# Kept weights in planes of 512 numbers per partition: transfers of 2 KB pieces in place of 8 and 4 KB

## The chip, the cores and the metric

The kernel runs on one core of a Trainium2 chip. The metric is the device time of one execution in microseconds, and the median of several runs is compared.

## The reference

A transformer block in float32 on x of 2 batches x 1024 tokens x 512. Only what matters here is shown:

```python
q = (x @ Wq.T)   # 32 heads of 128; x is layer-normed
k = (x @ Wk.T)   # 8 heads
v = (x @ Wv.T)
q = _rmsnorm(q, q_norm_w); k = _rmsnorm(k, k_norm_w)
scores = jnp.einsum('bkgqd,bksd->bkgqs', qg, k) / math.sqrt(HD)
attn = jax.nn.softmax(scores + bias[None], axis=-1)   # causal, ALiBi
out = jnp.einsum('bkgqs,bksd->bkgqd', attn, v)
x = x + out @ Wo.T
x = x + SCALING * einsum('bshr,hor,bsh->bso', low, B, scores)   # LoRA mixture of 8 experts on layernorm(x)
```

## The kernel before

**Work.** A group is one key/value head with its four query heads, in one batch: 8 groups for batch 0, 8 for batch 1, 16 in all (w = 0 to 15), each over eight tiles of 128 tokens (s = 0 to 7). A group projects k and v (256 columns) and q (512 columns), forms the scores against all keys so far, takes the softmax, multiplies with the values and adds its part of the output projection to `y` in SBUF. Every product is made three times, from operands split into an upper and a lower part (`_hi`, `_lo`; `split_product`, line 1026), so weights exist in two parts as well.

**Weights.** In the first eight groups the raw weights are loaded (2 KB per row), turned by TensorE (line 1113) and split by ScalarE (`high`, line 706) and VectorE (`low`, line 898). The turned parts are `wkvT` (4 chunks x 256 numbers per partition), `wqT` and `woT` (4 x 512). Since the second batch needs them again, `keep_wkv`, `keep_wq` and `keep_wo` write each group's two parts to DRAM (`wkv_kept`, `wq_kept`, `wo_kept`), and `back_wkv`, `back_wq` and `back_wo` read them back in groups 8 to 15 in place of loading and turning. All of them are issued from ScalarE's queue, hi and then lo. In SBUF a partition's part is contiguous, 8 KB (wkv: 4 KB), and so it is in DRAM. TensorE waits for a read-back by the semaphores `wkv_back`, `wq_back` and `wo_back`; `high` waits for a write-back (`wkv_spilled` and so on) before the buffer is written over in the next group.

**Probabilities through memory.** The products with the values need the probabilities turned. Most 128 x 128 tiles are turned by TensorE. The tiles of `MEMORY_TILES` (for s = 7 these are j = 4 to 7) go another way: `send_p` (line 557) writes them to `p_bounce` in DRAM, `fetch_p` (line 568) reads one (s, j) back as four DMAs of 64 KB, one per 32 partitions, in pieces of 32 numbers (128 B), into one of three buffers `p_raw`; VectorE finishes the turn (`flip_p`, line 907), ScalarE copies the upper part (line 714) and GpSimd makes the lower (line 805). `send_p` and `fetch_p` are issued from SyncE's queue.

**Order.** Every engine follows one written list per kind of group (`PROLOGUE`, `GROUP_A` for groups 0 to 6, `BOUNDARY`, `FIRST_B`, `GROUP_B`, `LAST`), each taking from it what is its own, in order; a wait holds up all that stands behind it on that engine. The part of `GROUP_A` around the change reads:

```python
"... values.7.0 high.kv.2 "
"values.7.1 keep_wq low.kv.2 turn.p.7.2 flip_p.7.4 q.9.0 upper_p.7.4 ..."
"high.p.7.3 low.p.7.2 flip_p.7.5 fetch_p.7.7 low.p.7.3 upper_p.7.5 flip_p.7.6 lower_p.7.5 turn.q.8 high.kv.3 "
"values.7.2 high.q.8 low.kv.3 inv_k values.7.3 keep_wkv low.q.8 values.7.4 add_y.5 values.7.5 upper_p.7.6 "
"flip_p.7.7 q.9.1 lower_p.7.6 norm_k upper_p.7.7 y.6 lower_p.7.7 values.7.6 add_y.6 turn.k.0 values.7.7 ..."
```

`y.s` (line 1026 into `y_ps`, 12 products) needs `add_y` of the tile before (line 955), since `y_ps` is one buffer; `add_y.5` stands behind `flip_p.7.6` on VectorE. `load_wo`, on ScalarE's queue, stands shortly before `keep_wq` and reads 1 MB in pieces of 2 KB. The load of Wq (`wq_v`) reads for a partition four pieces of 2 KB that lie 128 rows of 2 KB apart.

Of the kernel before, what the change touches and what calls it, by code (L numbers as in the profile page):

```python
# [11 lines left out]
F32 = mybir.dt.float32  # L12
# [3 lines left out]
P = 128  # L16
# [273 lines left out]
def attention_lora_block(nc, x, Wq, Wk, Wv, Wo, q_norm_w, k_norm_w, A, B, Wr, br, out):  # L290
    NB, S, DM = x.shape
    HD = q_norm_w.shape[0]
    H = Wq.shape[0] // HD
    NG = Wk.shape[0] // HD
    G = H // NG
    NE, RK, _ = A.shape
    NT = S // P
    C = DM // P
    W512 = G * HD
# [65 lines left out]
    turned, flipped, sends = [], [], [0, 0]  # L365
# [27 lines left out]
    with ExitStack() as ctx:  # L393
# [12 lines left out]
        wqT_hi = sb("wqT_hi", [P, C, W512], F32R)  # L406
        wqT_lo = sb("wqT_lo", [P, C, W512], F32R)
        wkvT_hi = sb("wkvT_hi", [P, C, 2 * HD], F32R)
        wkvT_lo = sb("wkvT_lo", [P, C, 2 * HD], F32R)
        woT_hi = sb("woT_hi", [P, G, DM], F32R)  # L410
# [68 lines left out]
                return probs[1][:, t // 2, (t % 2) * DM:(t % 2 + 1) * DM]  # L479
            return x_source(b, t)  # L480

        wkv_kept = nc.dram_tensor("wkv_kept", [NG, 2, P, C * 2 * HD], F32).ap()
        wq_kept = nc.dram_tensor("wq_kept", [NG, 2, P, C * W512], F32).ap()
        wo_kept = nc.dram_tensor("wo_kept", [NG, 2, P, G * DM], F32).ap()

        p_bounce = nc.dram_tensor("p_bounce", [2, NT, G, P, P], F32).ap()

# [119 lines left out]
        def _(act):  # L607
# [20 lines left out]

            def keep_wkv(w):
                after(act, "low", "wkv", w + 1, 1)  # L630
                act.dma_start(wkv_kept[w + 1, 0], wkvT_hi[:].rearrange("p c n -> p (c n)").bitcast(F32)).then_inc(wkv_spilled, 16)
                act.dma_start(wkv_kept[w + 1, 1], wkvT_lo[:].rearrange("p c n -> p (c n)").bitcast(F32)).then_inc(wkv_spilled, 16)

            def keep_wq(w):
                after(act, "low", "wq", w + 1, C - 1)
                act.dma_start(wq_kept[w + 1, 0], wqT_hi[:].rearrange("p c n -> p (c n)").bitcast(F32)).then_inc(wq_spilled, 16)
                act.dma_start(wq_kept[w + 1, 1], wqT_lo[:].rearrange("p c n -> p (c n)").bitcast(F32)).then_inc(wq_spilled, 16)

            def keep_wo(w):
                after(act, "low", "wo", w, G - 1)  # L640
                act.dma_start(wo_kept[w, 0], woT_hi[:].rearrange("p c n -> p (c n)").bitcast(F32)).then_inc(wo_spilled, 16)
                act.dma_start(wo_kept[w, 1], woT_lo[:].rearrange("p c n -> p (c n)").bitcast(F32)).then_inc(wo_spilled, 16)

            def back_wkv(w):
                g = w + 1 - NG
                after(act, "turn", "kv", w, C - 1)
                act.wait_ge(wkv_spilled, 32 * NG)
                act.dma_start(wkvT_hi[:].rearrange("p c n -> p (c n)").bitcast(F32), wkv_kept[g, 0]).then_inc(wkv_back, 16)
                act.dma_start(wkvT_lo[:].rearrange("p c n -> p (c n)").bitcast(F32), wkv_kept[g, 1]).then_inc(wkv_back, 16)

            def back_wq(w):
                g = w + 1 - NG
                after(act, "q", w, NT - 1, C - 1)
                act.wait_ge(wq_spilled, 32 * NG)
                act.dma_start(wqT_hi[:].rearrange("p c n -> p (c n)").bitcast(F32), wq_kept[g, 0]).then_inc(wq_back, 16)
                act.dma_start(wqT_lo[:].rearrange("p c n -> p (c n)").bitcast(F32), wq_kept[g, 1]).then_inc(wq_back, 16)

            def back_wo(w):
                g = w - NG
                after(act, "y", w - 1, NT - 1)  # L660
                act.wait_ge(wo_spilled, 32 * NG)
                act.dma_start(woT_hi[:].rearrange("p c n -> p (c n)").bitcast(F32), wo_kept[g, 0]).then_inc(wo_back, 16)
                act.dma_start(woT_lo[:].rearrange("p c n -> p (c n)").bitcast(F32), wo_kept[g, 1]).then_inc(wo_back, 16)

            def high(w, of, *which):
                name = named(w, "turn", of, *which)
# [544 lines left out]
```

## Time and profile before

| | |
|---|---|
| median of 3 runs | 2136.99 us (2133.37 to 2137.82) |
| the profiled execution's own time | 2138.16 us |
| its span in the profile | 2136.3 us, granted TensorE clock 0.993 |
| busy: TensorE, VectorE, ScalarE, GpSimd | 98%, 63%, 54%, 44% |
| chain that ended last | TensorE 83%, VectorE 4%, issue 4%, DMA 3% |
| DMA packets | 329,095, 176.81 MB |
| q1 (issued by SyncE) | 305,264 packets, 72.41 MB, 15.3% of 16 engines |
| q10 (issued by ScalarE) | 23,664 packets, 102.25 MB, 12.8% of 16 engines |

Times in the profile are microseconds from the start of the span. PE is TensorE, DVE VectorE, ACT ScalarE, POOL GpSimd, SP SyncE; a q behind an engine's name is its queue of instructions that don't occupy the engine. "A<-B" is what an instruction writes and reads. Idle time in brackets is the engine's own before that instruction, with what ended it. A DMA packet is one contiguous piece; the four bytes that raise a semaphore at the end of a DMA on each of the 16 DMA engines are counted as a packet too. "To landing" is from the issue to the semaphore's last step.

### The profile page before, as it was taken

The numbers are of one execution on the slowest core, as the hardware profiler recorded it, in microseconds if no ns is written. First come the engines' busy times: TensorE is split into PE (matmuls) and PEld (weight loads), VectorE is DVE, ScalarE is ACT, GpSimd is POOL, SyncE is SP. The second block draws the span as 40 slices with busy tenths as digits, with TensorE's granted clock in tenths as the row PEclk, the third lists the DMA queues.
The fourth block names the chain that finished last, engine by engine and source line by source line (L and its number), as shares of the span: only waits on it lengthen the run. The fifth ranks groups of instructions, "written<-read, shape, count | busy, mean of one in ns | idle before, by whom it ended". The sixth has DMA issues, their size and how long they took to land.

```text
span 2136.3 us, 33509 instructions
## 1 busy us (share of the span) xinstructions
PE 2083.0 (98%) x11772; PEld 1786.4 (84%) x11772; DVE 1355.6 (63%) x3431; ACT 1148.2 (54%) x3314; POOL 936.1 (44%) x984
## 2 busy tenths in 40 slices
PE   7999999999999999999999999999999999999997
PEld 6888888888888888888888888888888888888885
DVE  6656656566565665658876556566566656656676
ACT  4555545555454654645445555555555555555552
POOL 3443434444444443444443544435453443545443
PEclk9999999999999999999999999999999999999998
DMA  4152141511415125051350422313041231304112
GB/s 158 64 140 75 30 130 64 154 60 40 133 54 150 60 55 157 16 154 55 110 157 7 113 70 68 101 50 92 28 107 62 67 102 50 89 30 106 44 36 73
DMA packets 329095, 176.81 MB, mean 83 GB/s; under 512 B 243800, under 2 KB 301144, under 8 KB 320736
## 3 DMA queue, kind: packets, MB, share of 16 engines
q1 hardware_dynamic: 305264, 72.41, 15.3%
q10 hardware_dynamic: 23664, 102.25, 12.8%
q8 instruction: 95, 1.56, 0.3%
q14 instruction: 72, 0.59, 0.1%
HBM read 99.11 MB, written 75.50 MB: 82 GB/s over the span
## 4 chain that ended last, share of the span: by engine, by line
PE 83%; DVE 4%; issue 4%; DMA 3%; SPq 2%; POOL 2%; ACT 2%; ACTq 0%; DVEq 0%; POOLq 0%
PE s_ps L1026 17%; PE q_ps L1026 15%; PE y_ps L1026 15%; PE o_ps L1026 15%; PE turn_ps L1113 13%; PE turn_ps L1026 5%; DMA p_raw<-p_bounce 3%; SPq L568 2%; POOL probs_odd L799 1%; PE turn_ps L1107 1%; PE y_ps L1186 1%; DVE pT_lo L898 1%; DMA p_bounce<-probs_odd 1%; DVE y L955 0%; DVE oT_lo L949 0%
## 5 line engine op out<-in xcount | busy, mean ns | idle before, releaser
L799 POOL TENSOR_TENSOR probs_odd<-probs_odd,p_inv 128x256 f32<-128x256 f32 (+3 forms) x256 | 316.4, 1256 | 326.9 <-DVE p_inv L928 326.9
L706 ACT ACTIVATE pT_hi<-turn_ps 128x512 fp32r<-128x512 f32 x464 | 271.6, 597 | 316.2 <-PE turn_ps L1113 315.9
L799 POOL TENSOR_TENSOR probs_even<-probs_even,p_inv 128x128 f32<-128x128 f32 (+3 forms) x256 | 261.8, 1044 | 386.1 <-DVE p_inv L928 386.1
L898 DVE TENSOR_TENSOR pT_lo<-turn_ps,pT_hi 128x512 fp32r<-128x512 f32 x464 | 314.6, 684 | 146.2 <-ACT pT_hi L706 145.2
L921 DVE CUSTOM_DVE_ANT_0 probs_odd<-s_ps,rel 128x256 f32<-128x256 f32 (+3 forms) x256 | 209.3, 820 | 131.9 <-issue 131.4
L1026 PE MATMUL s_ps<-kT_hi,qT_hi 128*128 128x512 f32 (+3 forms) x768 | 278.7, 363 | 2.6 <-DVE kT_lo L900 1.8
L1026 PE MATMUL s_ps<-kT_hi,qT_lo 128*128 128x512 f32 (+3 forms) x768 | 262.9, 342 | 0.0
L1026 PE MATMUL s_ps<-kT_lo,qT_hi 128*128 128x512 f32 (+3 forms) x768 | 262.1, 341 | 0.0
L720 ACT ACTIVATE probs_odd<-probs_odd,neg_max 128x256 f32<-128x256 f32 (+3 forms) x256 | 211.9, 832 | 76.0 <-DVE neg_max L921 75.9
L921 DVE CUSTOM_DVE_ANT_0 probs_even<-s_ps,rel 128x128 f32<-128x128 f32 (+3 forms) x256 | 174.0, 686 | 118.0 <-issue 117.2
L1026 PE MATMUL o_ps<-pT_hi,v_hi 128*128 128x512 f32 x576 | 243.9, 423 | 1.9 <-DVE pT_lo L898 0.9
L1026 PE MATMUL q_ps<-wqT_hi,xnT_hi 128*128 128x512 f32 x512 | 220.9, 431 | 7.0 <-DVE qn L932 6.9
L1026 PE MATMUL o_ps<-pT_hi,v_lo 128*128 128x512 f32 x576 | 226.3, 393 | 0.0
L1026 PE MATMUL o_ps<-pT_lo,v_hi 128*128 128x512 f32 x576 | 226.0, 392 | 0.0
L720 ACT ACTIVATE probs_even<-probs_even,neg_max 128x128 f32<-128x128 f32 (+3 forms) x256 | 184.4, 721 | 76.6 <-DVE neg_max L921 75.7
L805 POOL TENSOR_TENSOR pT_lo<-p_raw,pT_hi 128x512 fp32r<-128x512 f32 x112 | 145.5, 1306 | 182.2 <-ACT pT_hi L714 181.5
L1026 PE MATMUL y_ps<-woT_hi,oT_hi 128*128 128x512 f32 x512 | 206.8, 404 | 18.7 <-DVE y L955 16.6
L1026 PE MATMUL y_ps<-woT_hi,oT_lo 128*128 128x512 f32 x512 | 203.2, 397 | 0.0
L1026 PE MATMUL y_ps<-woT_lo,oT_hi 128*128 128x512 f32 x512 | 202.5, 395 | 0.0
L1026 PE MATMUL q_ps<-wqT_hi,xnT_lo 128*128 128x512 f32 x512 | 201.4, 393 | 0.0
L1026 PE MATMUL q_ps<-wqT_lo,xnT_hi 128*128 128x512 f32 x512 | 200.6, 392 | 0.0
L1026 PEld LDWEIGHTS s_ps<-kT_hi,qT_hi 128*128 128x128 f32 x768 | 145.3, 189 | 22.3 <-DVE neg_max L921 2.1
(110 smaller groups left out, 4578.6 us busy)
## 6 DMA issues: line engine op xcount, KB each, us to landing
p_raw<-p_bounce SPq DMA_DIRECT2D x448, 64.0 KB, 2.3
p_bounce<-probs_odd SPq DMA_DIRECT2D x64, 256.0 KB, 2.3
wq_kept<-wqT_hi ACTq DMA_DIRECT2D x8, 1024.0 KB, 5.8
wq_kept<-wqT_lo ACTq DMA_DIRECT2D x8, 1024.0 KB, 8.4
wo_kept<-woT_hi ACTq DMA_DIRECT2D x8, 1024.0 KB, 8.1
wo_kept<-woT_lo ACTq DMA_DIRECT2D x8, 1024.0 KB, 10.2
p_bounce<-probs_even SPq DMA_DIRECT2D x64, 128.0 KB, 1.8
wqT_hi<-wq_kept ACTq DMA_DIRECT2D x8, 1024.0 KB, 4.8
```

Of the source, the lines that this page charges most:

```text
L568: sp.dma_start(p_raw[b * BLOCK:(b + 1) * BLOCK, n % RAW_TILES, :].rearrange("p (n j) -> p n j", j=BLOCK), blocks[b]).then_inc(p_fetched[n ...
L706: nc.scalar.activation(target, bank, ACT.Copy).then_inc(sems["high"], 1)
L720: nc.scalar.activation(row, row, ACT.Exp, bias=neg_max[:, s % 2, h:h + 1], scale=-1.0, accum_out=p_sum[:, s % 2, h:h + 1]).then_inc(sems[" ...
L799: nc.gpsimd.tensor_tensor(row, row, p_inv[:, s % 2, h:h + 1].to_broadcast((P, L)), ALU.mult).then_inc(sems["normalise"], 1)
L805: nc.gpsimd.tensor_tensor(pT_lo[:, r, :], p_raw[:, fetch_number[w, s, j] % RAW_TILES, :], pT_hi[:, r, :].bitcast(F32), ALU.subtract).then_ ...
L898: nc.vector.tensor_tensor(target, bank, upper.bitcast(F32), ALU.subtract).then_inc(sems["low"], 1)
L921: nc.vector.tensor_tensor_reduce(out=probs[s % 2][:, h, 0:L], in0=s_ps[:, at_col:at_col + L], in1=rel[:, S - L:S], scale=-float(slopes[w % ...
L1026: last = nc.tensor.matmul(target, a, m, start=start and i == 0 and k == 0, stop=stop and i == len(pairs) - 1 and k == 2)
L1107: last = nc.tensor.matmul(bank[:, 0:P + NE], f_x[:, t % 2, c * P:(c + 1) * P], arT[:, c, :], start=c == 0, stop=c == C - 1)
L1113: last = nc.tensor.transpose(bank[0:width, i * rows:(i + 1) * rows], source, ident[0:rows, 0:rows])
L1186: nc.tensor.matmul(y_ps[:], low_turned[:, t % 2, :], bT[:], start=True, stop=True).then_inc(sems["f_out"], 1)
```

## The change

The kept copies get another layout in DRAM: planes of 128 partitions x 512 numbers, one for each chunk of 512 numbers of a partition. A partition's part lies in four pieces of 2 KB (wkv: two pieces) that are 256 KB apart. The data in SBUF, the number of DMAs, their sizes, their places in the lists and all waits are as before.

```diff
--- before.py
+++ after.py
@@ -479,9 +479,16 @@
                 return probs[1][:, t // 2, (t % 2) * DM:(t % 2 + 1) * DM]
             return x_source(b, t)
 
-        wkv_kept = nc.dram_tensor("wkv_kept", [NG, 2, P, C * 2 * HD], F32).ap()
-        wq_kept = nc.dram_tensor("wq_kept", [NG, 2, P, C * W512], F32).ap()
-        wo_kept = nc.dram_tensor("wo_kept", [NG, 2, P, G * DM], F32).ap()
+
+        wkv_kept = nc.dram_tensor("wkv_kept", [NG, 2, C // 2, P, W512], F32).ap()
+        wq_kept = nc.dram_tensor("wq_kept", [NG, 2, C, P, W512], F32).ap()
+        wo_kept = nc.dram_tensor("wo_kept", [NG, 2, G, P, DM], F32).ap()
+
+        def pieces(kept, g, part):
+            return kept[g, part].rearrange("c p n -> p c n")
+
+        def pairs(turned):
+            return turned[:].rearrange("p (a c) n -> p a (c n)", c=2).bitcast(F32)
 
         p_bounce = nc.dram_tensor("p_bounce", [2, NT, G, P, P], F32).ap()
 
@@ -628,39 +635,39 @@
 
             def keep_wkv(w):
                 after(act, "low", "wkv", w + 1, 1)
-                act.dma_start(wkv_kept[w + 1, 0], wkvT_hi[:].rearrange("p c n -> p (c n)").bitcast(F32)).then_inc(wkv_spilled, 16)
-                act.dma_start(wkv_kept[w + 1, 1], wkvT_lo[:].rearrange("p c n -> p (c n)").bitcast(F32)).then_inc(wkv_spilled, 16)
+                act.dma_start(pieces(wkv_kept, w + 1, 0), pairs(wkvT_hi)).then_inc(wkv_spilled, 16)
+                act.dma_start(pieces(wkv_kept, w + 1, 1), pairs(wkvT_lo)).then_inc(wkv_spilled, 16)
 
             def keep_wq(w):
                 after(act, "low", "wq", w + 1, C - 1)
-                act.dma_start(wq_kept[w + 1, 0], wqT_hi[:].rearrange("p c n -> p (c n)").bitcast(F32)).then_inc(wq_spilled, 16)
-                act.dma_start(wq_kept[w + 1, 1], wqT_lo[:].rearrange("p c n -> p (c n)").bitcast(F32)).then_inc(wq_spilled, 16)
+                act.dma_start(pieces(wq_kept, w + 1, 0), wqT_hi[:].bitcast(F32)).then_inc(wq_spilled, 16)
+                act.dma_start(pieces(wq_kept, w + 1, 1), wqT_lo[:].bitcast(F32)).then_inc(wq_spilled, 16)
 
             def keep_wo(w):
                 after(act, "low", "wo", w, G - 1)
-                act.dma_start(wo_kept[w, 0], woT_hi[:].rearrange("p c n -> p (c n)").bitcast(F32)).then_inc(wo_spilled, 16)
-                act.dma_start(wo_kept[w, 1], woT_lo[:].rearrange("p c n -> p (c n)").bitcast(F32)).then_inc(wo_spilled, 16)
+                act.dma_start(pieces(wo_kept, w, 0), woT_hi[:].bitcast(F32)).then_inc(wo_spilled, 16)
+                act.dma_start(pieces(wo_kept, w, 1), woT_lo[:].bitcast(F32)).then_inc(wo_spilled, 16)
 
             def back_wkv(w):
                 g = w + 1 - NG
                 after(act, "turn", "kv", w, C - 1)
                 act.wait_ge(wkv_spilled, 32 * NG)
-                act.dma_start(wkvT_hi[:].rearrange("p c n -> p (c n)").bitcast(F32), wkv_kept[g, 0]).then_inc(wkv_back, 16)
-                act.dma_start(wkvT_lo[:].rearrange("p c n -> p (c n)").bitcast(F32), wkv_kept[g, 1]).then_inc(wkv_back, 16)
+                act.dma_start(pairs(wkvT_hi), pieces(wkv_kept, g, 0)).then_inc(wkv_back, 16)
+                act.dma_start(pairs(wkvT_lo), pieces(wkv_kept, g, 1)).then_inc(wkv_back, 16)
 
             def back_wq(w):
                 g = w + 1 - NG
                 after(act, "q", w, NT - 1, C - 1)
                 act.wait_ge(wq_spilled, 32 * NG)
-                act.dma_start(wqT_hi[:].rearrange("p c n -> p (c n)").bitcast(F32), wq_kept[g, 0]).then_inc(wq_back, 16)
-                act.dma_start(wqT_lo[:].rearrange("p c n -> p (c n)").bitcast(F32), wq_kept[g, 1]).then_inc(wq_back, 16)
+                act.dma_start(wqT_hi[:].bitcast(F32), pieces(wq_kept, g, 0)).then_inc(wq_back, 16)
+                act.dma_start(wqT_lo[:].bitcast(F32), pieces(wq_kept, g, 1)).then_inc(wq_back, 16)
 
             def back_wo(w):
                 g = w - NG
                 after(act, "y", w - 1, NT - 1)
                 act.wait_ge(wo_spilled, 32 * NG)
-                act.dma_start(woT_hi[:].rearrange("p c n -> p (c n)").bitcast(F32), wo_kept[g, 0]).then_inc(wo_back, 16)
-                act.dma_start(woT_lo[:].rearrange("p c n -> p (c n)").bitcast(F32), wo_kept[g, 1]).then_inc(wo_back, 16)
+                act.dma_start(woT_hi[:].bitcast(F32), pieces(wo_kept, g, 0)).then_inc(wo_back, 16)
+                act.dma_start(woT_lo[:].bitcast(F32), pieces(wo_kept, g, 1)).then_inc(wo_back, 16)
 
             def high(w, of, *which):
                 name = named(w, "turn", of, *which)
```

## Rows read from the trace of the kernel before

**Rows 1.** The page, part 1, whole span: busy us (share), instructions.

```profile
PE 2083.0 (98%) x11772; PEld 1786.4 (84%) x11772; DVE 1355.6 (63%) x3431; ACT 1148.2 (54%) x3314; POOL 936.1 (44%) x984
```

**Rows 2.** Who waited for whom, whole span: us, times, longest.

```profile
DVE p_raw L907 <- DMA p_raw<-p_bounce: 42.8, 18, 4.9
...
PE y_ps L1026 <- DVE y L955: 16.6, 7, 2.9
```

**Rows 3.** VectorE in time: start, us, instruction, idle before it.

```profile
160.31 0.71 DVE L907 STREAM_TRANSPOSE p_raw<-p_raw 128x512 f32<-128x512 f32 x1 [4.53 <-DMA p_raw<-p_bounce]
...
162.17 0.67 DVE L955 TENSOR_TENSOR y<-y_ps,y 128x512 f32<-128x512 f32 x1
...
949.74 0.71 DVE L907 STREAM_TRANSPOSE p_raw<-p_raw 128x512 f32<-128x512 f32 x1 [3.98 <-DMA p_raw<-p_bounce]
```

**Rows 4.** TensorE in time, the product after it.

```profile
162.99 0.47 PE L1026 MATMUL y_ps<-woT_hi,oT_hi 128*128 128x512 f32 x1 [2.58 <-DVE y L955]
```

**Rows 5.** ScalarE's queue in time, first group.

```profile
150.75 0.34 ACTq L636 DMA_DIRECT2D wq_kept<-wqT_hi  x1
...
151.12 0.45 ACTq L637 DMA_DIRECT2D wq_kept<-wqT_lo  x1
...
157.01 0.33 ACTq L631 DMA_DIRECT2D wkv_kept<-wkvT_hi  x1
```

**Rows 6.** SyncE's queue in time, same stretch.

```profile
149.69 10.57 SPq L568 DMA_DIRECT2D p_raw<-p_bounce  x6
```

**Rows 7.** DMA issues, 149.7 to 151.5, then 151.6 to 153.5: to landing.

```profile
p_raw<-p_bounce SPq DMA_DIRECT2D x1, 64.0 KB, 9.3
...
p_raw<-p_bounce SPq DMA_DIRECT2D x1, 64.0 KB, 8.7
```

**Rows 8.** DMA queues, 152.3 to 152.9: packets, MB, share of 16 engines.

```profile
q1 hardware_dynamic: 944, 0.12, 128.2%
...
q10 hardware_dynamic: 7, 0.02, 9.4%
```

**Rows 9.** DMA queues, 153.5 to 157.5.

```profile
q10 hardware_dynamic: 214, 1.62, 96.6%
q1 hardware_dynamic: 193, 0.02, 4.5%
```

**Rows 10.** DMA queues, 158.5 to 158.9.

```profile
q10 hardware_dynamic: 2, 0.01, 5.0%
```

**Rows 11.** DMA queues, 149.5 to 151.5.

```profile
q10 hardware_dynamic: 319, 0.65, 87.9%
q1 hardware_dynamic: 262, 0.03, 10.6%
```

**Rows 12.** DMA issues, whole span: count, KB each, median us to landing.

```profile
wqT_hi<-wq_kept ACTq DMA_DIRECT2D x8, 1024.0 KB, 4.8
wqT_lo<-wq_kept ACTq DMA_DIRECT2D x8, 1024.0 KB, 7.4
...
w_raw<-in_L_attn_Wq ACTq DMA_DIRECT2D x7, 1024.0 KB, 6.6
```

**Rows 13.** Read-backs and first uses in time: wkv, wq, wo.

```profile
1237.54 0.33 ACTq L648 DMA_DIRECT2D wkvT_hi<-wkv_kept  x1
...
1247.00 0.28 PE L1026 MATMUL turn_ps<-wkvT_hi,xnT_hi 128*128 128x256 f32 x1
...
1172.73 0.33 ACTq L655 DMA_DIRECT2D wqT_hi<-wq_kept  x1
...
1188.63 0.40 PE L1026 MATMUL q_ps<-wqT_hi,xnT_hi 128*128 128x512 f32 x1
...
1989.44 0.33 ACTq L662 DMA_DIRECT2D woT_hi<-wo_kept  x1
...
2003.17 0.39 PE L1026 MATMUL y_ps<-woT_hi,oT_hi 128*128 128x512 f32 x1
```

**Rows 14.** ScalarE in time, the next write to wkvT_hi.

```profile
181.93 0.60 ACT L706 ACTIVATE wkvT_hi<-turn_ps 128x512 fp32r<-128x512 f32 x1
```

## The prediction

> **What bounds the kernel now.** I read five views. First the busy times: TensorE works for 98% of the span [rows 1], so nothing that this change touches can matter unless TensorE comes to wait for it. Then who waits for whom: TensorE loses 16.6 us in seven waits at y_ps for the VectorE line that adds y_ps to y, and VectorE loses 42.8 us for the landing of p_raw [rows 2]. No wait of TensorE names a transfer of kept weights. Third, VectorE in time: in the first group it stands 4.53 us before the transpose of p_raw, and the addition to y, which is behind it in VectorE's written order, starts only at 162.17; the same stands in each of the seven groups with a write-back of wq, the last at 949.74 [rows 3]. TensorE's next y product starts at 162.99 after 2.58 us of idle time [rows 4]. So the seven stalls are 2.4 us each and have one cause, a fetch of the tile (s=7, j=6) that lands late.
>
> Fourth, the queues. ScalarE's queue issues the write-back of wq at 150.75 and 151.12 and that of wkv at 157.01 [rows 5], while SyncE's queue issues six fetches over 10.57 us [rows 6]. The two last quarters of the late tile land 9.3 and 8.7 us after their issues at 149.69 and 151.55, the last one at 160.28 [rows 7]. Fifth, the packets. Until 152.9 the ScalarE queue (q10) is all but empty, and q1 moves 944 packets in 0.6 us on 16 engines, 10 ns a packet on each [rows 8]. Then from 153.5 to 157.5 q10 starts 214 packets, 16 of which are counted by their 4 bytes in a semaphore, and q1 193: one for one [rows 9]. An 8 KB packet takes 0.966 x 64 us / 198 = 312 ns, a 128 B one 13 ns, so a fetch gets one small packet per 325 ns. From 158.5 to 158.9 q10 is empty again [rows 10], and there the fetches catch up.
>
> **The change, part by part.** It changes three transfers each way, 8 KB (wkv: 4 KB) packets into 2 KB ones. 40 MiB are written and 40 MiB read; that was 12,288 packets and becomes 40,960, 28,672 more. No wait, no engine instruction and no issue is added or moved.
>
> *Packet time.* The trace has 2 KB packets beside fetches, those of the Wo load just before: from 149.5 to 151.5, 319 of q10 at 87.9% and 262 of q1 [rows 11], that is 0.879 x 32 us / 319 = 88 ns each, against 78 ns for a quarter of an 8 KB one. A round of one and one is 101 ns, and in these two us q1 got 0.82 packets for one. Sixteen 8 KB packets per engine (2 MB of wq) take 5.0 us now; sixty-four of 2 KB take 5.6 us, 0.6 us more.
>
> *The collision.* At 152.9 two quarters of the late tile are outstanding. A quarter is 64 KB in 128 B pieces, 32 per engine and one semaphore, so 66 packets per engine. Now: 16 get through beside wq's 16 packets (16 x 325 ns, to 158.1), the other 50 run alone in the gap of rows 10 at 10 ns, to 158.6; with 0.5 us from last packet to landing, which I take as an estimate from a fetch's whole 1.9 us when nothing is beside it, that is 159.1. Measured is 160.28: the slowest of the 16 engines does not finish in the gap and is caught by wkv's packets. After: 66 rounds of 101 ns are 6.7 us, to 159.6, and no gap is left, since wq's write-back itself ends at about 159.3 and wkv's is queued behind it. Landing 160.1 on an average engine; some four packets more on the slowest give 160.5. So the small packets are served four times as often, but they need all the rounds that there are, and both queues end together. Against 160.28 this is +0.2 us a group, seven times +1.5 us. Bounds: if the slowest engine now loses its 1.2 us through 8 KB packets alone and later doesn't, 159.6, -0.7 us a group, -5 us; if q1 keeps the 0.82 of rows 11, 66 packets want 80 rounds of q10, 16 of them of wkv, 80 x 88 + 66 x 13 ns = 7.9 us, landing 161.3, +1.0 us, +7 us. I take +1.5 us, the value of one for one, because rows 9 show it over the longest stretch.
>
> *What is late next.* The following tile (s=7, j=7) is fetched behind it; it lands about 0.6 us later through the longer packets. y's product and one of o stand ahead of its use on TensorE, some 5 us. Cost nothing; without that cover at most 0.6 x 7 = 4 us.
>
> *Read-backs.* The Wq load has the very pattern that they get, 2 KB pieces 256 KB apart. It lands 6.6 us after its issue, the read-back of as much in 8 KB packets 4.8, and the second of a pair 7.4 [rows 12]. From above, two such loads one after the other are 13.6 us for a pair of wq or wo, 7.0 for wkv's pair, which has half the bytes. The slack: wkv is issued at 1237.54 and first used at 1247.00, 9.5 us; wq 1172.73 to 1188.63, 15.9; wo in the last group, where it is least, 1989.44 to 2003.17, 13.7 [rows 13]. All are covered, wo by 0.1 us at the bound and by some 4 us at the likelier 9.4 (6.6, and 32 pieces of 88 ns more); if cover failed it would be one wait per group.
>
> *Write-backs of wkv and wo.* wkv_hi is written over only at 181.93 [rows 14], 25 us after its issue; the others later still. Nothing.
>
> *Issuing.* ScalarE's queue spends 0.33 and 0.45 us on a pair. It may take longer with four times the pieces, but it stands in an engine that is busy 54% of the span [rows 1]; nothing, and the case that it blocks is a rival.
>
> Sum, against the profiled execution's 2138.16 us (span 2136.3): 2138.2 + 1.5 = 2139.7. That execution is 1.2 us above the median of the runs, 2136.99, so **2138.5 us**.
>
> The Trainium skill, DMA: Bandwidth & Descriptors, Queues, rings and completion order, says that an engine drains a whole packet of some 9 to 17 descriptors from one ring before it turns to the next. By that rule four to eight turns, not 66, would bring the fetch through, and it would land without delay before and after; rows 9 disagree with it, 193 against 198 single pieces.
>
> **Rivals.**
> *Faster: the fetch slips through beside the small packets.* For it: a small packet waits 88 ns in place of 312. If q1 gets 1.3 packets for one, 66 of them need 51 of q10, 51 x 88 + 66 x 13 = 5.3 us, landing 158.7, -1.6 us a group, 2127.5; with two for one or an engine that keeps several packets in flight the tile lands before 157.9, the stall of 2.4 us is gone whole, and -16.6 us give 2120.4. Against: in neither window does q1 get more than its one. Chance 0.22.
>
> *Slower: the pieces are dearer than 88 ns.* A partition's four pieces lie 256 KB apart, and the transfer of this kind in the trace needs 1.8 us more per MB than the 8 KB one [rows 12]. Over its 32 packets per engine these are 56 ns each. With the whole of it 66 rounds last 10.4 us, landing 163.8, +3.5 us x 7 = 2161.5; with half, 2149. Against: those are reads, whose first packets come slowly, while the packets from 149.5 on took 88 ns [rows 11]; the collision has writes. It decides from 9 ns per packet on (0.6 us a group, 4.3 us). Chance 0.15.
> The Trainium skill, DMA: Bandwidth & Descriptors, Latency and other measured facts, has copies at a row pitch of 512 KB run at 207 GB/s, about half of what the packets of rows 9 move (8 KB in 312 ns on 16 engines, 420 GB/s). No row here shows a write at such a pitch.
>
> *Slower: q1 lags as in rows 11.* 0.82 packets for one, 161.3, as above: 2144. Chance 0.10.
>
> *Slower: ScalarE's issues block as SyncE's do.* Six issues of SyncE took 10.57 us [rows 6], because four quarters hold 132 pieces per engine. ScalarE will have at most 99 outstanding (a load and two write-backs). If it blocked 1.5 us in each of 24 write-backs beside loads and a third reached TensorE, +12 us, 2150. Chance 0.03.
>
> *The change doesn't do what it says*: the pieces are joined again, and nothing moves. Chance 0.02, within no change.
>
> **The numbers.** Forecast with both its bounds 0.48. A difference under 0.2%, 4.3 us, can't be told from none. Faster: the first rival 0.22, less 0.02 that falls inside, and 0.02 of the forecast's lower bound: 0.22. Slower: 0.15 + 0.10 + 0.03, and the forecast's upper edge is mostly inside: 0.28. The rest, 0.50. The range takes in the first rival at its half (2127.5) and a little more, and the second at its half (2149): 2125 to 2150.
>
> **What would show it.** In the changed profile: 2 KB packets alone in q10, 28,672 more of them; between the starts of the wq write-back and its end q1 and q10 one for one at about 100 ns a round, some 5.5 to 6.5 us long; no empty q10 before wkv's packets; the tile's last quarter landing 8.5 to 9.5 us after its issue (now 8.7); TensorE's waits at y_ps still seven, 14 to 20 us in sum; p_raw's wait on VectorE 38 to 50 us; read-backs landing 6 to 7 and 9 to 10 us after issue with no wait on them. I am wrong if the seven stalls shrink below 10 us or grow over 25, if TensorE waits for a read-back, or if ScalarE's issues last over 1 us.

## The result and the profile after

The changed kernel takes 2141.8 us (median of 20 runs, 2137.26 to 2145.53) against 2137.96 for the kernel before (20 runs, 2133.37 to 2143.22): a ratio of 1.0018 [1.0011, 1.0026], 3.8 us more. The brackets hold the 95% interval, which leaves out 1, so the loss is small but clear of the noise. The forecast was no change that can be told, with +1.5 us as its sum. The profiled execution took 2139.75 us (span 2137.9).

Line numbers are 7 higher than before: the split product is L1033, the addition to `y` L962, `flip_p` L914, `fetch_p` L575. Four lines of the page of the changed kernel: busy times, the packets of the whole span, and the two queues:

```profile
PE 2080.4 (97%) x11772; PEld 1784.0 (83%) x11772; DVE 1356.4 (63%) x3431; ACT 1149.1 (54%) x3314; POOL 936.1 (44%) x984
...
DMA packets 357767, 176.81 MB, mean 83 GB/s; under 512 B 243800, under 2 KB 301144, under 8 KB 357600
...
q1 hardware_dynamic: 305264, 72.41, 15.4%
q10 hardware_dynamic: 52336, 102.25, 13.5%
```

q10 has 52,336 packets in place of 23,664, which is the 28,672 more that were counted, for the same bytes; its share of the 16 engines rises from 12.8% to 13.5%.

Who waited for whom, changed kernel (us in total, times, longest):

```profile
DVE p_raw L914 <- DMA p_raw<-p_bounce: 46.0, 22, 5.5
...
PE y_ps L1033 <- DVE y L962: 20.1, 7, 3.5
```

These answer to [rows 2]: the same seven stalls of TensorE, 20.1 us in place of 16.6, so +3.5 us. No line names a read-back.

VectorE and then TensorE in time, first group (start, us, instruction, idle before it), to be read against [rows 3, 4]:

```profile
159.38 0.71 DVE L914 STREAM_TRANSPOSE p_raw<-p_raw 128x512 f32<-128x512 f32 x1 [5.01 <-DMA p_raw<-p_bounce]
...
161.24 0.68 DVE L962 TENSOR_TENSOR y<-y_ps,y 128x512 f32<-128x512 f32 x1
```

```profile
162.06 0.64 PE L1033 MATMUL y_ps<-woT_hi,oT_hi 128*128 128x512 f32 x1 [3.34 <-DVE y L962]
```

The chain is the old one: VectorE stands before the transpose of the late tile, 5.01 us in place of 4.53, the addition waits behind it, and TensorE loses 3.34 us in place of 2.58. The seven stalls of after are 3.34, 3.50, 2.76, 3.28, 3.13, 2.11 and 2.03 us, those of before 2.58, 2.95, 2.46, 2.91, 1.79, 1.87 and 2.03.

The landing explains them. Measured from the issue of wq's write-back, which takes out that the groups start at other times, the late tile's last quarter lands after 10.3, 10.5, 9.7, 10.2, 10.1, 9.1 and 9.0 us (mean 9.83), before after 9.5, 9.9, 9.4, 9.9, 8.7, 8.8 and 9.0 (mean 9.32). That is 0.51 us a group, 3.6 us for seven: the 3.5 us of the wait.

The landing of the write-back itself goes with it. In every group the late quarter lands just behind wq's lower half: 0.34 to 0.51 us behind it in the kernel before, 0.15 to 0.35 us in the changed one. That half lands a mean 8.93 us after the first half's issue before and 9.64 after, 0.71 later. So in both kernels the fetch ends when the write-back does.

Two queues of the changed kernel, first group: 151.9 to 156.9, then the first and the last 2.5 us of it, and the microsecond behind (packets, MB, share of 16 engines):

```profile
q10 hardware_dynamic: 919, 1.84, 94.9%
q1 hardware_dynamic: 771, 0.10, 12.9%
...
q10 hardware_dynamic: 476, 0.95, 98.5%
q1 hardware_dynamic: 233, 0.03, 8.4%
...
q10 hardware_dynamic: 443, 0.89, 91.4%
q1 hardware_dynamic: 538, 0.07, 17.4%
...
q1 hardware_dynamic: 1092, 0.14, 87.8%
q10 hardware_dynamic: 83, 0.15, 38.9%
```

A 2 KB packet takes 0.985 x 2.5 x 16 us / 476 = 83 ns. Over the whole collision q1 gets 771 packets for 919, 0.84 for one. But the share isn't even: 0.49 in the first half, 1.2 in the second. Then there is a gap in q10 before wkv's packets, and q1 makes up for much of it there, with 1,092 packets in 1 us.

The kernel before is as uneven, which the average of [rows 9] hides. These are its queues from 153.5 to 155.0 and from 155.0 to 157.5:

```profile
q10 hardware_dynamic: 74, 0.61, 96.8%
q1 hardware_dynamic: 31, 0.00, 3.3%
...
q10 hardware_dynamic: 140, 1.02, 96.4%
q1 hardware_dynamic: 162, 0.02, 5.3%
```

Read-backs and write-backs (DMA issues, whole span: count, KB, median us to landing):

```profile
wq_kept<-wqT_hi ACTq DMA_DIRECT2D x8, 1024.0 KB, 6.0
wq_kept<-wqT_lo ACTq DMA_DIRECT2D x8, 1024.0 KB, 9.3
...
wqT_hi<-wq_kept ACTq DMA_DIRECT2D x8, 1024.0 KB, 5.8
wqT_lo<-wq_kept ACTq DMA_DIRECT2D x8, 1024.0 KB, 8.4
...
wkvT_hi<-wkv_kept ACTq DMA_DIRECT2D x8, 512.0 KB, 3.6
wkvT_lo<-wkv_kept ACTq DMA_DIRECT2D x8, 512.0 KB, 4.5
```

wq's read-back is 1.0 us later in each half than in [rows 12]. It has 15.9 us of slack [rows 13].

A second cost shows in the clock. Stretches of 4.5 us from a stalled y product on, of the kernel before (groups 1 and 3), then of the changed kernel (group 3); columns: us, busy time and instructions of PE, PEld, DVE, ACT, POOL, granted clock, DMA share, GB/s:

```profile
163.00:167.50 4.50, 4.50 (x13) 3.56 (x14) 1.82 (x2) 0.63 (x1) 1.52 (x2) 0.62 0.01 2
427.60:432.10 4.50, 4.49 (x21) 3.63 (x22) 2.51 (x3) 0.99 (x2) 1.56 (x2) 1.00 0.01 2
```

```profile
427.50:432.00 4.50, 4.48 (x13) 3.57 (x14) 1.82 (x2) 0.63 (x1) 1.56 (x2) 0.62 0.02 4
```

After some of the stalls TensorE runs about 3.4 us at its lower level, 1.2 GHz, and makes 13 products where it makes 21 at 2.4 GHz: 8 products of 0.22 us, 1.7 us lost beside the stall itself. Before, this followed four of the seven stalls (those of 2.58, 2.95, 2.91 and 1.87 us), after, five (the first five). So in the stretch of the seven stalls the change costs 3.5 us of waiting and 1.7 us of clock, 5.2 us. The issues of wq's write-back confirm it: from that of the first group to that of the seventh 789.98 us pass before and 794.97 after, 5.0 us more.

The two profiled executions still differ by only 1.6 us, because the kernel before was at the lower level for longer where the kernels don't differ in code. Once it was so in the first group; 40.5 to 43.9 us, before and then after, same columns:

```profile
40.50:43.90 3.40, 3.40 (x18) 3.40 (x18) 2.55 (x9) 1.47 (x5) 0.00 (x0) 0.50 1.01 417
```

```profile
40.50:43.90 3.40, 3.40 (x28) 3.17 (x28) 3.40 (x16) 2.13 (x8) 0.05 (x1) 1.00 1.03 384
```

The changed kernel issues its first group's write-back 1.7 us sooner (149.06 against 150.75). The other place is the end of the span; last 36.3 us of before and last 37.9 us of after:

```profile
2100.00:2136.30 36.30, 23.96 (x98) 15.89 (x97) 19.40 (x50) 5.79 (x14) 6.51 (x8) 0.81 0.19 52
```

```profile
2100.00:2137.90 37.90, 25.25 (x117) 17.09 (x115) 21.11 (x52) 6.96 (x16) 6.52 (x8) 0.92 0.25 60
```

(1 - 0.81) x 36.3 x 2 = 13.8 us at the lower level against (1 - 0.92) x 37.9 x 2 = 6.1 us, 7.7 us less, worth at most 3.9 us. From the seventh write-back to the end of the span the changed kernel takes 1193.9 us against 1195.6, 1.7 us less. The three parts give 5.0 - 1.7 - 1.7 = 1.6. So 3.4 us of the 5.0 were hidden in this pair by chance. The measured 3.8 us of the medians lie between 1.6 and 5.0.

### The profile page after: what moved, and what is told of

It reads as the page before. It is cut to its first block, busy times and chain, and to the rows that moved or that the text cites. A ratio compares the mean times of both kernels' runs of the same rounds, so it can differ in the third digit from the quotient of the medians.

```text
span 2137.9 us, 33509 instructions
## 1 busy us (share of the span) xinstructions
PE 2080.4 (97%) x11772; PEld 1784.0 (83%) x11772; DVE 1356.4 (63%) x3431; ACT 1149.1 (54%) x3314; POOL 936.1 (44%) x984
## 3 DMA queue, kind: packets, MB, share of 16 engines
q10 hardware_dynamic: 52336, 102.25, 13.5%
## 4 chain that ended last, share of the span: by engine, by line
PE 83%; DVE 4%; issue 4%; DMA 3%; SPq 2%; POOL 2%; ACT 2%; ACTq 0%; POOLq 0%; DVEq 0%
PE s_ps L1033 17%; PE q_ps L1033 15%; PE y_ps L1033 15%; PE o_ps L1033 15%; PE turn_ps L1120 13%; PE turn_ps L1033 5%; DMA p_raw<-p_bounce 3%; SPq L575 2%; POOL probs_odd L806 1%; DVE pT_lo L905 1%; PE turn_ps L1114 1%; PE y_ps L1193 1%; DMA p_bounce<-probs_odd 1%; DVE y L962 0%; DVE oT_lo L956 0%
## 5 line engine op out<-in xcount | busy, mean ns | idle before, releaser
L1033 PE MATMUL s_ps<-kT_hi,qT_hi 128*128 128x512 f32 (+3 forms) x768 | 278.1, 362 | 2.6 <-DVE kT_lo L907 1.8
L1033 PE MATMUL s_ps<-kT_hi,qT_lo 128*128 128x512 f32 (+3 forms) x768 | 262.4, 342 | 0.0
L1033 PE MATMUL s_ps<-kT_lo,qT_hi 128*128 128x512 f32 (+3 forms) x768 | 261.6, 341 | 0.0
L1033 PE MATMUL o_ps<-pT_hi,v_hi 128*128 128x512 f32 x576 | 243.9, 423 | 1.7 <-DVE pT_lo L905 0.9
L1033 PE MATMUL y_ps<-woT_hi,oT_hi 128*128 128x512 f32 x512 | 207.2, 405 | 22.3 <-DVE y L962 20.1
L1033 PE MATMUL q_ps<-wqT_hi,xnT_hi 128*128 128x512 f32 x512 | 220.8, 431 | 7.0 <-DVE qn L939 6.9
L1033 PE MATMUL o_ps<-pT_hi,v_lo 128*128 128x512 f32 x576 | 226.3, 393 | 0.0
L1033 PE MATMUL o_ps<-pT_lo,v_hi 128*128 128x512 f32 x576 | 226.0, 392 | 0.0
L1033 PE MATMUL y_ps<-woT_hi,oT_lo 128*128 128x512 f32 x512 | 203.6, 398 | 0.0
L1033 PE MATMUL y_ps<-woT_lo,oT_hi 128*128 128x512 f32 x512 | 203.1, 397 | 0.0
L1033 PE MATMUL q_ps<-wqT_hi,xnT_lo 128*128 128x512 f32 x512 | 201.3, 393 | 0.0
L1033 PE MATMUL q_ps<-wqT_lo,xnT_hi 128*128 128x512 f32 x512 | 200.5, 392 | 0.0
L1033 PEld LDWEIGHTS s_ps<-kT_hi,qT_hi 128*128 128x128 f32 x768 | 144.8, 189 | 22.3 <-DVE neg_max L928 2.2
## 6 DMA issues: line engine op xcount, KB each, us to landing
wo_kept<-woT_lo ACTq DMA_DIRECT2D x8, 1024.0 KB, 10.1
```

What stands on the lines that cost most here:

```text
L1033: last = nc.tensor.matmul(target, a, m, start=start and i == 0 and k == 0, stop=stop and i == len(pairs) - 1 and k == 2)
```

## The experiments

Every ratio is against the kernel before, run on the same chip beside it. "Waits at y_ps" are the seven of TensorE. The theory that came out of the result: the loss is the collision of wq's write-back with the late fetch, and the other transfers cost nothing.

**1. Which transfers cost: e1_wq_planes and e2_wkv_wo_planes.** The first puts only wq in planes, the second only wkv and wo.

```diff
--- after.py
+++ e1_wq_planes.py
-        wkv_kept = nc.dram_tensor("wkv_kept", [NG, 2, C // 2, P, W512], F32).ap()
-        wo_kept = nc.dram_tensor("wo_kept", [NG, 2, G, P, DM], F32).ap()
+        wkv_kept = nc.dram_tensor("wkv_kept", [NG, 2, P, C * 2 * HD], F32).ap()
+        wo_kept = nc.dram_tensor("wo_kept", [NG, 2, P, G * DM], F32).ap()
...
--- after.py
+++ e2_wkv_wo_planes.py
-        wq_kept = nc.dram_tensor("wq_kept", [NG, 2, C, P, W512], F32).ap()
+        wq_kept = nc.dram_tensor("wq_kept", [NG, 2, P, C * W512], F32).ap()
...
```

> Only wq's copies are in planes; wkv and wo stay contiguous (4 and 8 KB packets). Theory A (the loss is the wq write-back beside the late fetch): the whole of the change's loss or nearly, +2 to +4 us against before, the seven waits of TensorE at y_ps 19 to 20.5 us in sum, last quarter of the tile about 9.8 us after the write-back's issue. Theory B (the read-backs, or 28,672 packets spread over the run, cost it): about +1 us, in proportion to wq's share of the packets, and the seven waits stay at 16.6 us. Theory C (wkv's small packets behind catch the fetch): no loss, waits 16.6 us.

> wkv's and wo's copies are in planes, wq's stay contiguous in 8 KB packets. Theory A: no difference from before, the seven waits 16 to 17 us. Theory B: most of the loss, +2 us or more, elsewhere than in the seven waits. Theory C: the seven waits grow by 1 to 4 us, since the wkv packets that catch the slowest engine come in twice the number.

wq alone: 2141.89 us (11 runs) against 2138.28, ratio 1.0015 [1.0007, 1.0024], 3.6 us of the 3.8. wkv and wo alone: 2138.46, ratio 1.0002 [0.9993, 1.001]. Their waits at y_ps, in this order:

```profile
PE y_ps L1033 <- DVE y L962: 20.7, 7, 4.4
```

```profile
PE y_ps L1033 <- DVE y L962: 16.4, 7, 3.0
```

The loss is wq's, as far as it can be told; wkv and wo, write-backs and read-backs, were costed at nothing, and their interval reaches from -1.5 to +2.1 us. The first version's longest stall, 4.4 us, is in its first group. There the late quarter lands at 160.75, after q1 had next to nothing beside wkv's write-back, DMA queues from 158.5 to 160:

```profile
q10 hardware_dynamic: 173, 0.63, 102.1%
q1 hardware_dynamic: 14, 0.00, 0.8%
```

In its fourth group, where the stall is 3.11 us, the last quarter is issued at 548.57, between the two halves of wq's write-back (548.28 and 548.70). DMA queues from 551.3 to 553.8:

```profile
q10 hardware_dynamic: 511, 1.02, 104.7%
q1 hardware_dynamic: 17, 0.00, 0.5%
```

For 2.5 us q1 gets one packet for thirty. That isn't one for one; experiment 6 comes back to it.

**2. Is it the pitch: e3_padded_rows.** 2 KB pieces of a partition 2,304 B apart in place of 256 KB.

```diff
--- after.py
+++ e3_padded_rows.py
+        wq_kept = nc.dram_tensor("wq_kept", [NG, 2, P, C, W512 + 64], F32).ap()
...
-            return kept[g, part].rearrange("c p n -> p c n")
+            return kept[g, part][:, :, 0:W512]
```

> All copies in 2 KB pieces, but a partition's four pieces lie 2304 B apart in one row, not 256 KB apart in planes. Theory A, where only the packet's size matters: as the changed kernel, +3 to +5 us against before, seven waits near 20 us. Theory D (the distance of 256 KB makes pieces dear): as before, 16 to 17 us of waits.

2141.23 us (12 runs), ratio 1.0018 [1.001, 1.0027], the changed kernel's own; waits at y_ps 20.7 us. The distance between the pieces plays no part that can be told, only their size. The Trainium skill, DMA: Bandwidth & Descriptors, Latency and other measured facts, gives 207 GB/s for copies at a row pitch of 512 KB, 164 at 2 MB, and calls 214 the full rate of these copies; so by that page 512 KB costs little, and at 256 KB and for 2 KB pieces no loss shows here.

**3. How size counts: e5_4kb and e4_1kb.**

```diff
--- after.py
+++ e4_1kb.py
-        wq_kept = nc.dram_tensor("wq_kept", [NG, 2, C, P, W512], F32).ap()
+        wq_kept = nc.dram_tensor("wq_kept", [NG, 2, 8, P, 256], F32).ap()
...
--- after.py
+++ e5_4kb.py
-        wq_kept = nc.dram_tensor("wq_kept", [NG, 2, C, P, W512], F32).ap()
+        wq_kept = nc.dram_tensor("wq_kept", [NG, 2, 2, P, 1024], F32).ap()
...
```

> Planes of 256 numbers, so pieces of 1 KB. A packet should take some 48 ns (88 ns at 2 KB and 312 at 8 KB give 37 ns per KB and 10 fixed), a round with a small one 61 ns. Theory A with one packet for one: the wq write-back has 128 rounds per engine, and the 66 packets of the late fetch are through after 4.0 us, landing at 157.5 in the first group: the stalls vanish, -10 to -16 us against before. Theory E (what costs is the number of packets, every further one delays the fetch): the waits grow again, 24 us or more, +8 us. Theory F (the fetch gets no turn in the first 1 to 2 us of the write-back whatever the size, then one for one): waits 8 to 14 us, -3 to -8 us.

> Planes of 1024 numbers for wq and wo, pieces of 4 KB; wkv's stay one piece of 4 KB. A round is 160 + 13 ns, wq's write-back has 32 per engine and lasts 5.5 us; 32 of the 66 small packets go beside it and the rest in the gap behind. Theory A: the landing is that of the kernel before, waits 15.5 to 18 us, the time within 0.1% of before (2138). Theory E (loss grows with the number of packets): waits 18 us or more, +1 to +2 us.

| pieces | us | ratio | waits at y_ps | last quarter, mean |
|---|---|---|---|---|
| 8 KB (before) | 2138.0 | 1 | 16.6 | 9.3 |
| 4 KB | 2139.37 | 1.0006 [0.9996, 1.0015] | 18.6 | 9.6 |
| 2 KB (after) | 2141.8 | 1.0018 [1.0011, 1.0026] | 20.1 | 9.8 |
| 1 KB | 2140.17 | 1.0005 [0.9996, 1.0013] | 14.1 | 9.0 |

4 KB lies between, as a growing cost of the packets would have it; its waits are just above the 18 us of theory A, and its time can't be told from either neighbour's. 1 KB breaks the row: the fetch does get through sooner, 0.8 us of the 2 KB landing, and now 0.8 to 2.5 us before wq's lower half. But the stalls at y_ps shrink by 2.5 us against before and not by the 10 to 16 of turns one for one, and TensorE waits later in its list in return, where k is turned. This line has no counterpart in the kernel before:

```profile
PE turn_ps L1120 <- issue: 2.9, 3, 1.6
```

In the first group the stall is 1.6 us at y_ps and 1.6 us there. So what the fetch gains is lost again behind it. From the first write-back of wq to the seventh the kernel with 1 KB takes 790.0 us, that before 790.0, with 4 KB 792.5, with 2 KB 795.0 (one execution each).

**4. Move the write-backs out of the way: m_before_both and m_after_both.** `keep_wkv` goes behind `high.q.2` and `keep_wq` behind `high.p.5.0` in `GROUP_A`; the data are complete at both places. Once with the old layout, once with the new one.

```diff
--- before.py
+++ m_before_both.py
-    "values.0.0 exp.1.1 low.wkv.0 q.3.0 max.1.2 turn.q.2 invert.1.0 low.wkv.1 normalise.1.0 q.3.1 high.q.2 max.1.3 "
+    "values.0.0 exp.1.1 low.wkv.0 q.3.0 max.1.2 turn.q.2 invert.1.0 low.wkv.1 normalise.1.0 q.3.1 high.q.2 keep_wkv max.1.3 "
...
-    "scores.6.1 high.wq.3 low.wq.3 turn.p.5.0 max.6.1 turn.p.5.1 fetch_p.5.5 high.p.5.0 q.8.0 high.p.5.1 o_low.4 "
+    "scores.6.1 high.wq.3 low.wq.3 turn.p.5.0 max.6.1 turn.p.5.1 fetch_p.5.5 high.p.5.0 keep_wq q.8.0 high.p.5.1 o_low.4 "
...
-    "values.7.1 keep_wq low.kv.2 turn.p.7.2 flip_p.7.4 q.9.0 upper_p.7.4 turn.p.7.3 high.p.7.2 turn.kv.3 lower_p.7.4 "
+    "values.7.1 low.kv.2 turn.p.7.2 flip_p.7.4 q.9.0 upper_p.7.4 turn.p.7.3 high.p.7.2 turn.kv.3 lower_p.7.4 "
...
-    "values.7.2 high.q.8 low.kv.3 inv_k values.7.3 keep_wkv low.q.8 values.7.4 add_y.5 values.7.5 upper_p.7.6 "
+    "values.7.2 high.q.8 low.kv.3 inv_k values.7.3 low.q.8 values.7.4 add_y.5 values.7.5 upper_p.7.6 "
```

> The kernel before (8 and 4 KB packets) with both write-backs of the first-batch groups issued earlier in ScalarE's list, wkv's at about 50 us into the group and wq's at about 110 us, away from the fetches of s = 7. Theory A (the seven stalls are this collision): the seven waits at y_ps go from 16.6 us to under 2, and the time falls by 13 to 17 us, to about 2122. Rival G (the Wo load alone is enough to hold the fetch up): waits of 8 us or more stay, -8 us at most. Rival H (the wq write-back now delays the fetches of s = 5 and 6): a new wait of TensorE there, and less than half of the gain.

> The changed kernel (2 KB pieces) with the same two write-backs moved in the same way. Theory A: the change's loss is gone together with the stalls, so the time is that of m_before_both within 1.5 us. Theory B (2 KB pieces cost something by themselves): 3 to 5 us above m_before_both.

2111.36 us (4 runs) against 2137.28, ratio 0.9883 [0.9867, 0.9898]; with the new layout 2110.2, ratio 0.9879 [0.9865, 0.9892]. Busy times and VectorE's wait in the first of the two:

```profile
PE 2073.6 (98%) x11772; PEld 1781.5 (84%) x11772; DVE 1360.4 (64%) x3431; ACT 1149.8 (54%) x3314; POOL 942.1 (45%) x984
```

```profile
DVE p_raw L907 <- DMA p_raw<-p_bounce: 4.2, 11, 0.8
```

The wait at y_ps isn't among its lines any more, and p_raw's is 4.2 us in place of 42.8. The 26 us come out of the rows: 16.6 us of waits, and TensorE busy 9.4 us less (2083.0 to 2073.6) for the same products, 6.8 of it the clock after four stalls; the rest wasn't traced. With the collision gone the planes are 1.2 us faster (4 runs each), not slower, which shows that the loss was in the collision. Both versions beat both kernels by at least 1.2%, far more than the layout cost. The moved write-back still collides with fetches there: in the first group those of the tile s = 5 land up to 9.0 us after its issue, but nothing waits for them.

**5. Is it wkv's packets that catch the slowest engine: m_before_wkv and m_after_wkv.** Only `keep_wkv` is moved, to its place of experiment 4.

```diff
--- before.py
+++ m_before_wkv.py
-    "values.0.0 exp.1.1 low.wkv.0 q.3.0 max.1.2 turn.q.2 invert.1.0 low.wkv.1 normalise.1.0 q.3.1 high.q.2 max.1.3 "
+    "values.0.0 exp.1.1 low.wkv.0 q.3.0 max.1.2 turn.q.2 invert.1.0 low.wkv.1 normalise.1.0 q.3.1 high.q.2 keep_wkv max.1.3 "
...
-    "values.7.2 high.q.8 low.kv.3 inv_k values.7.3 keep_wkv low.q.8 values.7.4 add_y.5 values.7.5 upper_p.7.6 "
+    "values.7.2 high.q.8 low.kv.3 inv_k values.7.3 low.q.8 values.7.4 add_y.5 values.7.5 upper_p.7.6 "
```

> The kernel before, with only wkv's write-back moved early; wq's stays where it was. Theory C' (in the kernel before the slowest DMA engine is caught by wkv's packets, which is 1.2 us of each landing): the last quarter lands about 8.3 us after the wq write-back's issue in place of 9.3, the seven waits sum to 9 to 11 us in place of 16.6, -5 to -8 us. If wkv plays no part: waits 16 us, no difference.

> The changed kernel, with only wkv's write-back moved early. With theory C' and one packet for one: the fetch needs nearly all rounds of wq's write-back anyway, so it gains less than the kernel before, 0.3 to 0.7 us a group: waits 15 to 18 us, -2 to -5 us against the changed kernel (2141.8), so about 2138. If wkv plays no part: 2141.8.

2134.21 us against 2137.28, ratio 0.9992 [0.9984, 1.0001], waits at y_ps 17.3 us; with planes 2140.12, ratio 1.0013 [1.0004, 1.0022], waits 20.7. Without wkv's packets the last quarter lands 9.4 us after wq's issue in the old layout (9.3 with them), and 9.9 with planes (9.8). So on average they don't delay it, and the loss of the planes stays, 5.9 us between these two. A single group can still be hit, as the first one of e1_wq_planes was. What does go is part of p_raw's wait, 42.8 to 33.5 us, which is the next tile's, and TensorE doesn't wait for that one.

**6. What order of issue does: e6_lo_later, s_before_wq_later and s_after_wq_later.** The first issues the lower half of wq's write-back 2.5 us later, with planes. The others move the whole of `keep_wq` behind `high.p.7.3`, where both quarters of the late tile are issued ahead of it, with the old layout and with planes.

```diff
--- after.py
+++ e6_lo_later.py
-    "high.p.7.3 low.p.7.2 flip_p.7.5 fetch_p.7.7 low.p.7.3 upper_p.7.5 flip_p.7.6 lower_p.7.5 turn.q.8 high.kv.3 "
+    "high.p.7.3 keep_wqlo low.p.7.2 flip_p.7.5 fetch_p.7.7 low.p.7.3 upper_p.7.5 flip_p.7.6 lower_p.7.5 turn.q.8 high.kv.3 "
...
+                if w < 0:
+                    keep_wqlo(w)
+
+            def keep_wqlo(w):
...
--- before.py
+++ s_before_wq_later.py
-    "values.7.1 keep_wq low.kv.2 turn.p.7.2 flip_p.7.4 q.9.0 upper_p.7.4 turn.p.7.3 high.p.7.2 turn.kv.3 lower_p.7.4 "
-    "high.p.7.3 low.p.7.2 flip_p.7.5 fetch_p.7.7 low.p.7.3 upper_p.7.5 flip_p.7.6 lower_p.7.5 turn.q.8 high.kv.3 "
+    "values.7.1 low.kv.2 turn.p.7.2 flip_p.7.4 q.9.0 upper_p.7.4 turn.p.7.3 high.p.7.2 turn.kv.3 lower_p.7.4 "
+    "high.p.7.3 keep_wq low.p.7.2 flip_p.7.5 fetch_p.7.7 low.p.7.3 upper_p.7.5 flip_p.7.6 lower_p.7.5 turn.q.8 high.kv.3 "
```

> The changed kernel; only the second half of wq's write-back (the lo part) is issued about 3 us later, behind the issue of the last quarter of the late fetch; the first half stays. Theory I (descriptors of both queues pass through one place in the order of issue, so the last quarter's are held up behind the write-back's 64 per engine, which is why q1 stands at 0 to 20 packets per 0.5 us for 1 to 3 us while a quarter is issued and not landed): no such stretch is left, q1 and q10 are one for one from the write-back's first packet, the last quarter lands at most 9.4 us after the write-back's issue in place of 9.84 on average, the waits at y_ps fall from 20 to 16 us or less. Rival J (the two queues only take turns on each DMA engine, and the empty stretches are something else): the stretches stay, waits 19 to 21 us.

> The kernel before, with wq's write-back issued about 3 us later, behind the last quarter of the late fetch and before the fetch of the next tile; wkv's stays. Theory A: the late fetch of (7, 6) goes alone and lands by 155, its stall of 2.4 us goes; now the fetch of (7, 7) runs beside 8 KB packets and lands 2 to 3 us later, at 166 to 167, and a new wait of TensorE of 0 to 2 us a group stands before the last product with the values. Time -12 to -22 us against before. Rival K (any write-back among the fetches costs the same stall, wherever): within 4 us of before.

> The changed kernel with the same move. The fetch of (7, 7) has 132 packets per engine beside 64 of wq's and 32 of wkv's, of 2 KB. One for one it needs 132 rounds whatever stands beside, and both queues end together: its landing within 1 us of that in s_before_wq_later, and the time within 3 us of it. If small pieces let the fetch through: 3 us or more below it; if the number of pieces holds it up: 3 us or more above.

e6_lo_later: 2140.72 us (11 runs), ratio 1.0014 [1.0003, 1.0024]. TensorE's waits:

```profile
PE y_ps L1037 <- DVE y L966: 11.6, 4, 5.3
PE turn_ps L1124 <- issue: 8.7, 4, 2.5
```

In four of the seven groups the last quarter lands 6.2 to 7.2 us after the upper half's issue, in the other three 9.6 to 12.3; where it lands early, a later wait takes the stall's place. Neither expectation is met in full: the waits at y_ps fall to 11.6 us, but with those at turn_ps they are 20.3. The run settles nothing but that a stall can change places within the group.

Both late write-backs lose, where a gain was expected: 2149.53 us (5 runs), ratio 1.005 [1.0038, 1.0063], and 2152.43 (5 runs), ratio 1.0063 [1.005, 1.0077]. Waits of the old layout's version, then VectorE in time, then its queues from 155.0 to 157.5:

```profile
PE turn_ps L1113 <- issue: 21.6, 7, 4.1
```

```profile
158.37 0.68 DVE L955 TENSOR_TENSOR y<-y_ps,y 128x512 f32<-128x512 f32 x1
164.10 0.71 DVE L907 STREAM_TRANSPOSE p_raw<-p_raw 128x512 f32<-128x512 f32 x1 [5.05 <-DMA p_raw<-p_bounce]
```

```profile
q10 hardware_dynamic: 143, 1.05, 105.4%
q1 hardware_dynamic: 9, 0.00, 0.3%
```

The tile (7, 6) is in time, and the addition starts at 158.37, 3.8 us sooner than in [rows 3]. But now the next tile (7, 7) is late: its quarters of 154.70 and 155.05, issued 1.1 and 1.5 us after the write-back (153.59), land at 160.67 and 160.98, its last at 164.08. VectorE stands 5.05 us for it. Its multiplication of k stands behind that transpose and ends at 165.92, and TensorE, which turns k next, starts at 166.02; it waits so seven times. From 155.0 to 157.5 q1 gets 9 packets. Such empty stretches, with 0 to 12 packets of q1 in all, last 2.0 to 4.8 us in the seven groups, and 3.0 to 4.5 us with 2 KB pieces. In the first group, old layout from 155.09 to 159.09 and then 2 KB pieces from 155.29 to 159.04:

```profile
q10 hardware_dynamic: 204, 1.54, 100.5%
q1 hardware_dynamic: 3, 0.00, 0.1%
```

```profile
q10 hardware_dynamic: 733, 1.47, 104.0%
q1 hardware_dynamic: 12, 0.00, 0.3%
```

So a fetch issued just behind the write-back gets next to nothing for as long with small pieces as with large, while q10 moves 1.1 to 1.8 of its 2 MB (0.7 in two of the groups with 8 KB). In pieces the two stretches are far apart, 13 and 46 per engine. The planes add 2.9 us here (2149.53 to 2152.43), as they do at the old place.

## Why the prediction held, and what in it didn't

**The number** came out within the forecast in part by luck. The loss of 3.8 us is 0.5 us short of the 4.3 that the prediction took for the smallest difference that can be told; with 20 runs of each kernel the interval is some 1.6 us to either side, so the loss was told from none. In the stretch of the stalls the traces show 5.0 us.

**What bounds the kernel** stands: the same seven stalls, the same chain behind the fetch of (7, 6). With the write-back moved the stalls are gone. But the case was priced too low: 16.6 us were the waits alone, and taking the collision out gives 26 us, most of the rest through the clock, which fell after four of the seven stalls.

**Packet count and packet time** stand: 28,672 more, 83 ns against the 88 taken from the load of Wo.

**The collision** is the step that was mis-sized. It said 66 rounds of one and one, 101 ns each, and +0.2 us a group, +1.5 us in all; measured are 0.51 us a group and 3.5 us. q1 didn't get one for one but 0.84 over the write-back, close to the 0.82 of [rows 11] that I took as the bound (+1.0 us a group) and not as the value. I preferred [rows 9] because they were the longest stretch, but their 193 for 198 is an average of 31 for 74 in the first 1.5 us and 162 for 124 in the rest (16 of the 140 are semaphores). The errors of rate and gap partly cancel.

**The gap.** "No gap is left" was wrong: q1 gets 1,092 packets in one us before wkv's packets start, and much of what it had missed is made good there. That is the likely reason why 0.84 gave half of its bound.

**The slowest engine caught by wkv's packets** was the reason given for 1.2 us of the landing before. Experiment 5 refutes it: with wkv moved away the landing is the same. I had put a remainder down to the nearest thing. What the rows show in its place is the end of wq's own write-back. The prediction let the fetch of the kernel before finish in the gap on an average engine and only that of the changed one end with the write-back; both do. In 46 of the 49 groups of the seven kernels with 8 or 2 KB pieces for wq and its write-back at the old place, the late quarter lands 0.15 to 0.51 us behind wq's lower half. By the prediction's own packet times the write-back lasts 0.6 us longer in 2 KB pieces (5.0 to 5.6 us), near the 0.51 by which the fetch is later. That the one causes the other is argued from this and not tested by itself; at 1 KB the fetch is free of it.

**Not in the sum**: 1.7 us for the one more stretch at 1.2 GHz. [rows 4] shows the stall, but I didn't look at how long the products behind it took. How many of seven stalls are followed by one differs between executions: 4, 3 and 3 with 8 KB (before, e2_wkv_wo_planes, m_before_wkv), 5, 5, 5 and 4 with 2 KB (after, e1_wq_planes, e3_padded_rows, m_after_wkv), where one in each of e1_wq_planes and m_after_wkv lasts 6.8 us.

**Read-backs, write-backs of wkv and wo, the pitch, the issues** were costed at nothing, and experiments 1 and 2 show no cost. Read-backs land after 5.8 and 8.4 us where 6 to 7 and 9 to 10 were thought likely. ScalarE's issues last 0.38 and 0.72 us in the first group in place of 0.34 and 0.45. Three last over the 1 us that I had named as a sign of being wrong: 1.47 us at 24.4, 1.12 at 554.1 and 1.02 at 719.0. The first has its like before (1.51 us), and no wait of TensorE names them. The 10.57 us of [rows 6] aren't all issue either: from 153.57 to 154.77 SyncE waits for a free buffer, and the six issues last 0.30 to 2.42 us each, 9.15 in all.

**The rivals.** "Slips through" is out at 2 and 4 KB, and hardly there at 1 KB (14.1 us of waits). "Dearer pieces" is out by the padded rows and by 83 ns. "q1 lags at 0.82" was right in its rate and too high in its price, since it left out the gap: 2144 against 2141.8. The first rival's 2127.5 should read 2125.8: seven times -1.6 us from 2137.0 and not from the forecast.

The Trainium skill, DMA: Bandwidth & Descriptors, Queues, rings and completion order, has a queue drain a packet of typically 9 to 17 descriptors, at most 64, before the other gets its turn. From this I let the fetch come through without delay, but q10's packets would take their time too, 3 to 5 us for 9 to 17 pieces of 312 ns. The trace disagrees with the typical packet in the second half of the write-back, where q1 and q10 alternate in small numbers (538 to 443), and in the empty stretches, where q10 starts 32 (511 in experiment 1) and 46 pieces per engine (733 in experiment 6) with next to nothing of q1.

The 207 GB/s that stood beside the rival of dearer pieces didn't speak for it: by the page of the Trainium skill that is named in experiment 3, the full rate of these copies is 214.

**Still open** is what holds q1 back while a write-back begins. The runs show when it happens (fetches issued behind it) and that packet size doesn't cure it; the cause wasn't found.

## What to carry to other kernels

Where a bulk transfer meets a small one for which an engine waits, its place counts and its packet size hardly: moving the write-backs was worth 26 us, packets of 1 to 8 KB differ by less than 4 us. To price an idle stall, look at the duration of the instructions behind it too, since TensorE may come back at half its clock. And read the rate of a shared queue in short pieces from the collision's first packet on: an average of one for one over 4 us hid a start of 31 packets for 74.

## What the runs showed of the hardware

- Fetches issued between or just behind the halves of a 2 MB write-back of another queue got 9 packets in 2.5 us at 8 KB pieces, 17 at 2 KB, beside 143 and 511 of the write-back; later they took turns of about one for one.
- A 64 KB fetch of 128 B pieces beside that write-back landed 0.15 to 0.51 us behind its lower half in 46 of 49 groups, with 8 KB and with 2 KB pieces.
- After stalls of 1.87 to 3.50 us TensorE ran some 3.4 us at 1.2 GHz, 13 products in 4.5 us in place of 21; after others of 1.79 to 3.07 us it didn't. The one of 3.07 us is in the second group of e1_wq_planes, with the 4.5 us behind it:

```profile
297.10:301.60 4.50, 4.47 (x21) 3.68 (x22) 2.51 (x3) 0.97 (x2) 1.57 (x2) 1.00 0.01 2
```

- The planes' 256 KB pitch cost nothing that can be told: 2141.23 us with pieces 2,304 B apart, 2141.8 with them, both 1.0018 of the kernel before.
